# Deferring the prefix's state update of a gated-linear-attention kernel behind the next supertile's gate head

## What is computed

```python
xn = layernorm(x)
q, k, v = xn @ Wq, xn @ Wk, xn @ Wv             # 1024, 1024, 2048 wide
g = log_sigmoid(xn @ Wgk1 @ Wgk2 + bgk2) / 16   # low-rank decay gate, rank 16
# per head, in chunks: bc = cumsum(g) inside the chunk, b_last its last row
A = mask((q*exp(bc)*scale) @ (k*exp(-bc)).T)
o = A @ v + (q*exp(bc)*scale) @ S
S = S * exp(b_last) + (k*exp(b_last - bc)).T @ v
attn = (rmsnorm(o) * silu(xn @ Wg)) @ Wo
moe  = sum over the top 2 of 4 experts of  w_e * LN(relu(LN(xn @ W1_e)) @ W2_e)  + xn
out  = x + attn + moe
```

## Time and profile before

| | us |
|---|---|
| median of 2 runs | 2765.34 |
| the runs | 2757.32, 2773.36 |
| profiled execution | 2758.54 |
| its span (slowest core, core 1) | 2757.0 |
| spans of the cores | 2737.4 to 2757.0 |

### The profile page before, as it was taken

One profiled execution on the slowest core, in us unless ns is written; L12 is line 12 of the kernel. 1 busy time (PEld: TensorE's weight loads), 2 busy tenths in 40 slices (PEclk: granted clock), 3 DMA queues, 4 the chain that ended last, 5 costly groups with the idle time before them and its releaser, 6 DMA issues.

```text
span 2757.0 us, 25311 instructions; the slowest of 8 cores (2737.4 to 2757.0 us)
## 1 busy us (share of the span) xinstructions
PE 1547.7 (56%) x6272; PEld 585.3 (21%) x6272; DVE 951.4 (35%) x2139; ACT 881.1 (32%) x1617; POOL 106.9 (4%) x152
## 2 busy tenths in 40 slices
PE   1390529153788156549776662199236556966850
PEld 0140104011333012213222220044112212322310
DVE  2433343343402332333245252421233331253253
ACT  2411641063124222204453433313322212533531
POOL 1000000000000000000010000000000001000000
PEclk9595859585899588869888875599678877988975
DMA  8051226112164201027373643034310004635323
GB/s 126 0 77 31 40 39 92 31 32 31 16 92 64 44 18 21 16 37 116 55 119 65 107 63 114 23 46 67 60 27 16 16 16 69 100 66 87 57 37 122
DMA packets 258284, 155.31 MB, mean 56 GB/s; under 512 B 173016, under 2 KB 242648, under 8 KB 258144
## 3 DMA queue, kind: packets, MB, share of 16 engines
q0 software_dynamic: 84576, 94.96, 22.8%
q1 hardware_dynamic: 168960, 41.96, 8.6%
q10 hardware_dynamic: 4608, 16.78, 1.8%
HBM read 198.04 MB, written 8.39 MB: 75 GB/s over the span
## 4 chain that ended last, share of the span: by engine, by line
PE 50%; DVE 20%; DMA 11%; issue 9%; ACT 7%; DVEq 2%; SPq 1%; ACTq 0%; POOL 0%; POOLq 0%
PE pa L291 20%; PE pb L291 19%; PE pf L291 7%; DVE s_bb L546 4%; DMA s_kgT<-s_kgs 4%; DVE s_kgs L668 2%; DMA s_gx<-x_tm 2%; DMA s_ogf<-s_ogc 2%; ACT s_sg L470 2%; DVEq L64 2%; PE pd L291 1%; PE pc L291 1%; DVE s_z L926 1%; DVE s_z L932 1%; DMA s_w<-W 1%
## 5 line engine op out<-in xcount | busy, mean ns | idle before, releaser
L291 PE MATMUL pa<-s_w,s_xn 128*128 128x512 bf16 x1280 | 331.6, 406 | 391.4 <-DVE s_v L638 238.2
L291 PE MATMUL pb<-s_w,s_xn 128*128 128x512 bf16 x1280 | 313.8, 389 | 5.6 <-DMA s_w<-W 5.6
L291 PEld LDWEIGHTS pa<-s_w,s_xn 128*128 128x128 bf16 x1280 | 124.9, 102 | 562.0 <-issue 441.1
L291 PE MATMUL pf<-s_w,s_ogf 128*128 128x512 bf16 x512 | 148.5, 462 | 123.4 <-DMA s_ogf<-s_ogc 123.4
L291 PE MATMUL pa<-s_w,s_hfm 128*128 128x512 bf16 x512 | 128.2, 395 | 74.0 <-DMA s_hfm<-s_h 64.1
L765 ACT ACTIVATE s_jb<-s_ogc 128x512 bf16<-128x512 bf16 x64 | 40.3, 630 | 394.3 <-DVE s_ogc L759 392.2
L291 PEld LDWEIGHTS pb<-s_w,s_xn 128*128 128x128 bf16 x1280 | 123.2, 100 | 167.4 <-issue 39.6
L546 DVE TENSOR_TENSOR_SCAN s_bb<-c_os,s_bb 128x128 f32<-128x128 f32 x256 | 108.8, 425 | 108.7 <-ACT s_bb L539 82.8
L846 DVE TENSOR_TENSOR s_mcol<-s_scol 128x8 f32<-128x8 f32 x16 | 2.7, 167 | 405.5 <-ACT s_jb L906 404.9
L668 DVE TENSOR_SCALAR s_kgs<-s_kd,s_eb 128x128 bf16<-128x128 bf16 x256 | 65.2, 255 | 170.1 <-DMA s_kgT<-s_kgs 111.5
L291 PE MATMUL pb<-s_w,s_hfm 128*128 128x512 bf16 x512 | 122.6, 382 | 0.0
(11 more groups left out here) (176 smaller groups left out, 2264.4 us busy)
## 6 DMA issues: line engine op xcount, KB each, us to landing
s_w<-W POOLq DMA_DIRECT2D x32, 1024.0 KB, 13.8
s_w<-Wv_p POOLq DMA_DIRECT2D x8, 1024.0 KB, 20.1
s_w<-Wv POOLq DMA_DIRECT2D x8, 1024.0 KB, 16.7
s_w<-Wg POOLq DMA_DIRECT2D x8, 1024.0 KB, 13.1
s_w<-Wo POOLq DMA_DIRECT2D x8, 1024.0 KB, 12.4
s_gx<-x_tm ACTq DMA_DIRECT2D x16, 512.0 KB, 4.2
out<-s_jf ACTq DMA_DIRECT2D x16, 512.0 KB, 2.9
s_xt<-xp_tm POOLq DMA_DIRECT2D x4, 1024.0 KB, 10.7
```

Source lines behind the costliest of these rows:

```text
L291: ret = e.matmul(out=o, lhsT=l, rhs=r, start=st, stop=sp)
```

## The change

It does four things.

1. `stage_DE(True, ...)` of a prefix supertile isn't emitted at the end of its own loop round. It is held in `pend_pDE` and emitted by `emit_pend_pDE` as `mid` of the next supertile's stage B: behind the sigmoids (in m0 behind the expert gate), before Ln and the scans. In m0 it is reached through `emit_pend_G`.
2. `s_eb` gets two copies, chosen by `epar`, so that stage B of the next supertile can write its own while the old one is held.
3. `s_diag` and `s_wgk2` get places of their own (`jb_off + 4096`, `jb_off + 2048`), and the row of ones shrinks from 512 to 128 elements, of which no more were used.
4. `load_B_smalls` also waits for ScalarE, `(sc, sc.n)`; as `stage_DE` is no longer emitted ahead of it, its wait for TensorE in p1 and m0 is one for stage C.

```diff
--- before.py
+++ after.py
@@ -180,8 +180,8 @@
     s_AT = alloc("s_AT", [128, H, 128], BF16, at=jb_off + 1024)
     s_rb2 = alloc("s_rb2", [1, 1024], BF16,
                   at=big0 + attn_sz + DV * 2 + 2048)
-    s_diag = alloc("s_diag", [128, NKC, 128], BF16, at=jb_off + 2048 + 1024)
-    s_wgk2 = alloc("s_wgk2", [16, NKC, 128], BF16, at=jb_off + 2048 + 1024)
+    s_diag = alloc("s_diag", [128, NKC, 128], BF16, at=jb_off + 4096)
+    s_wgk2 = alloc("s_wgk2", [16, NKC, 128], BF16, at=jb_off + 2048)
 
     wslot = [alloc(f"s_w{i}", [128, 4096], BF16) for i in range(4)]
 
@@ -209,7 +209,7 @@
     s_cf = alloc("s_cf", [128, 1024], F32, at=si0 + 16384 + 8192)
     s_jf = alloc("s_jf", [128, 1024], F32, at=si0 + 16384 + 8192 + 4096)
 
-    s_eb = alloc("s_eb", [128, NKC, NCH], F32)
+    s_eb = alloc("s_eb", [128, 2, NKC, NCH], F32)
     s_cols = alloc("s_cols", [128, 2, 8, NTC], F32)
     s_mcol = alloc("s_mcol", [128, 2, 4, NTC], F32)
     s_gsc = alloc("s_gsc", [128, 96], F32)
@@ -225,7 +225,7 @@
     c_idb = alloc("c_idb", [128, 128], BF16)
     c_mU = alloc("c_mU", [128, 128], F32)
     c_os = alloc("c_os", [128, 128], F32)
-    c_or1 = alloc("c_or1", [1, 512], BF16)
+    c_or1 = alloc("c_or1", [1, 128], BF16)
     s_gateb = alloc("s_gateb", [1, NE], BF16)
     s_cv = alloc("s_cv", [128, 3], F32)
     assert cur[0] <= BASE + 207 * 1024, f"SBUF arena overflow: {cur[0] - BASE}"
@@ -341,7 +341,7 @@
     g_dma(c_os[:, :], onescan)
     g_dma(s_cv[:, :], cvals)
     g_dma(s_rms[:, :], rms_c)
-    g_dma(c_or1[0:1, :], onesrow)
+    g_dma(c_or1[0:1, :], onesrow[0:1, 0:128])
     g_dma(s_gateb[:, :], gatebr)
     cm = gd.n
     v_op(lambda e: e.memset(s_S[:, :, :], 0.0), wait=[(gd, cm)])
@@ -422,7 +422,7 @@
 
     def load_B_smalls(smalls, gate):
         wgk1d, wgk2d, bgk2d = smalls
-        pre = [(gd, gd.n), (te, te.n)]
+        pre = [(gd, gd.n), (te, te.n), (sc, sc.n)]
         g_dma(s_wgk1[:, :, :],
               wgk1d.rearrange("p (c n) -> p c n", n=LR), wait=pre)
         g_dma(s_wgk2[:, :, :], wgk2d.rearrange("k (c n) -> k c n", n=128))
@@ -432,7 +432,7 @@
                   gateW.rearrange("p (c n) -> p c n", n=NE))
         return gd.n
 
-    def stage_B(gw, gate, xnm, stop=None, mid=None):
+    def stage_B(gw, gate, xnm, epar=0, stop=None, mid=None):
         if stop == "Bs":
             return None, None
         if gate:
@@ -555,7 +555,7 @@
                 wait=[(ve, bbok_h)] + ([(te, te.n), (tp, tp.n)] if hf == 0 else []))
             emms.append((sc, sc.n))
             s_op(lambda e, hf=hf: e.activation(
-                out=s_eb[:, hf * 4:(hf + 1) * 4, :],
+                out=s_eb[:, epar, hf * 4:(hf + 1) * 4, :],
                 in_=s_bb[:, hf * 4:(hf + 1) * 4, 127::128],
                 func=ACT.Exp, scale=1.0 / GN))
         for hf in range(2):
@@ -649,7 +649,7 @@
                 wu_done(slot)
 
     def stage_C(prefix, eq_marks, em_marks, pre=(None, None),
-                ded=(None, None)):
+                ded=(None, None), epar=0):
         vm = (te, te.n)
         proj_tm(s_v, Wv_p if prefix else Wv, None, vm, pre_slot=pre[0],
                 ded=ded[0])
@@ -668,7 +668,8 @@
                 v_op(lambda e, kc=kc, c=c: e.tensor_scalar(
                     out=s_kgs[:, c * 128:(c + 1) * 128],
                     in0=s_kd[:, kc, c * 128:(c + 1) * 128],
-                    scalar1=s_eb[:, kc, c:c + 1], scalar2=None, op0=ALU.mult),
+                    scalar1=s_eb[:, epar, kc, c:c + 1], scalar2=None,
+                    op0=ALU.mult),
                     wait=[(ve, ve.n), (tp, prev_tp)] +
                          ([eq_marks[1], (tg[0], tg[0].n), (tg[1], tg[1].n)]
                           if (kc == 0 and c == 0) else []))
@@ -678,7 +679,7 @@
             tpms.append((tp, tp.n))
         return tpms, qbm, kbm
 
-    def stage_DE(prefix, tpms, qbm=None, kbm=None):
+    def stage_DE(prefix, tpms, qbm=None, kbm=None, epar=0):
         tp0 = tp.n
         xd0 = xd.n
         ebm = sc.n
@@ -712,7 +713,8 @@
                 if c == 0 and r == 0:
                     w0 = w0 + [(sc, ebm)]
                 v_op(lambda e, r=r, c=c: e.tensor_scalar(
-                    out=s_diag[:, r, :], in0=c_idb[:, :], scalar1=s_eb[:, r, c:c + 1],
+                    out=s_diag[:, r, :], in0=c_idb[:, :],
+                    scalar1=s_eb[:, epar, r, c:c + 1],
                     scalar2=None, op0=ALU.mult), wait=w0)
             return ve.n
 
@@ -1126,12 +1128,19 @@
         cpar_of[("m", st)] = gi % 2
         gi += 1
     xnm = stage_A(xp_tm, 0, cpar_of[("p", 0)])
+    pend_pDE = [None]
+
+    def emit_pend_pDE():
+        if pend_pDE[0] is not None:
+            stage_DE(True, pend_pDE[0][0], epar=pend_pDE[0][1])
+            pend_pDE[0] = None
     for st in range(cfg.NPST):
+        cpar = cpar_of[("p", st)]
         pv = wu_next(Wv_p[:, 0:512])
         gw_ = load_B_smalls((Wgk1_p, Wgk2_p, bgk2c_p), gate=False)
-        r_ = stage_B(gw_, gate=False, xnm=xnm)
+        r_ = stage_B(gw_, gate=False, xnm=xnm, epar=cpar, mid=emit_pend_pDE)
         eqm, emm = r_
-        tpms, qbm_, kbm_ = stage_C(True, eqm, emm, pre=(pv, None))
+        tpms, qbm_, kbm_ = stage_C(True, eqm, emm, pre=(pv, None), epar=cpar)
         sqw = [(ve, ve.n)]
         if st + 1 < cfg.NPST:
             nsrc, nt0, ncp = xp_tm, (st + 1) * ST, cpar_of[("p", st + 1)]
@@ -1140,10 +1149,11 @@
         blks = [stage_A_blk(nsrc, nt0, b, ncp, (), sq_w=sqw)
                 for b in range(NBLK)]
         xnm = stage_A_xpose(blks, (te, te.n))
-        stage_DE(True, tpms)
+        pend_pDE[0] = (tpms, cpar)
     pend_G = [None]
 
     def emit_pend_G():
+        emit_pend_pDE()
         if pend_G[0] is not None:
             stage_G(*pend_G[0])
             pend_G[0] = None
@@ -1164,15 +1174,16 @@
         r_ = stage_B(gw_, gate=True, xnm=xnm,
                      stop=stop if (stop in ("Bw1", "Bw2", "Bw3", "Bs", "B0", "B1",
                                             "B2", "B3", "B4") and st >= stop_st)
-                     else None, mid=emit_pend_G)
+                     else None, mid=emit_pend_G, epar=cpar)
         if stop in ("B", "Bw1", "Bw2", "Bw3", "Bs", "B0", "B1", "B2", "B3", "B4") \
                 and st >= stop_st:
             break
         eqm, emm = r_
-        tpms, qbm_, kbm_ = stage_C(False, eqm, emm, pre=(pv, pg2), ded=dedv)
+        tpms, qbm_, kbm_ = stage_C(False, eqm, emm, pre=(pv, pg2), ded=dedv,
+                                   epar=cpar)
         if stop == "C" and st >= stop_st:
             break
-        stage_DE(False, tpms, qbm_, kbm_)
+        stage_DE(False, tpms, qbm_, kbm_, epar=cpar)
         if stop == "D" and st >= stop_st:
             break
         side = None
```

More of the change, by code:

```diff
@@ L1232, in build @@
         pairs = [("xn", s_xn[:, :, :]), ("bb", s_bb[:, :, :]),
-                 ("eb", s_eb[:, :, :]), ("qg", s_qg[:, :, :]),
+                 ("eb", s_eb[:, 0, :, :]), ("qg", s_qg[:, :, :]),
                  ("kd", s_kd[:, :, :]), ("kgT", s_kgT[:, :, :, :]),
```

## The result

| | before | after |
|---|---|---|
| median, us | 2765.71 (10 runs) | 2796.33 (11 runs) |
| ratio, 95% interval | | 1.0131, 1.0112 to 1.015 |
| profiled execution, us | 2758.54 | 2796.95 |
| its span, us | 2757.0 (core 1) | 2795.3 (core 5) |

The changed kernel takes 1.3% longer, 31 us of median and 38 us between the profiled executions. That is less than 2%, but the interval of the ratio leaves out 1: the kernel did get slower. 2795 was forecast. The slowest core is another one in the two profiles; core 5 of the kernel before took 2756.9 us, and from here on both kernels are read on core 5, where a comparison needs the same core. Medians over few runs can hold an execution disturbed by the chip; the ratios leave these out, and where a kernel has no ratio its profiled execution is quoted.

What follows compares the result with a forecast made beforehand. TensorE's waits were read as the bound, the change touching the stretches from stage C to the next Ln. First stage A +1.5, p0/p1 +19.9, p1/m0 +14.5, m1 0: +36 on 2758.5, forecast 2795 us, range 2758 to 2812.

Steps and rivals of the forecast that it cites:

- The order: At p0/p1 and p1/m0 the update changes places with the gate head, still in series, beside no scan or V projection.
- rival 5: Update and scans overlap after all: some 40 us less at each boundary, 2680 us; chance 0.02.
- The swap: Small loads stop waiting for the update, TensorE waits for the transposes: Ln +2.9 us at p0/p1, +2.5 at p1/m0.
- The loads: Weight loads issued ahead of block 1's four transposes delay the last landing: 17 us at p0/p1, 12 at p1/m0.
- the test: The loads-plus-transposes sum tried on the old first stage A: 63.6 against 60.71 us landed, 3 us heavy.
- The sharing of the queues: DMA engines go round their queues packet by packet, so three weight loads let three transposes through; p0/p1 landing at 315.7.
- Rival 3: Level or faster: transposes come first, 2750 us, or share time evenly, 2763; chance 0.12.
- The first stage A: Small loads wait for ScalarE's Exp, weights and block 1's transposes end together: +4.3 us, corrected to +1.5.
- Rival 2: Transposes partly starved: half of 14 us won in the first stage A, boundaries lose 12 and 8; 2777 us, chance 0.18.
- m1: Small loads wait for ScalarE's end of stage F, 1633.20 for 1629.64, hidden behind the expert mix: 0 us.
- The sum: First stage A +1.5, p0/p1 +19.9, p1/m0 +14.5, m1 0: +36 us, giving 2795.
- The signs: Changed profile: wait before the head on `s_xn`, none on `s_bgk`; transposes 10 us or more; Ln near 384 and 693.

Runs made afterwards that it cites:

- overlap kernel: Changed kernel with Ln issued ahead of the update, eight scans behind each chunk's diagonal tiles, tiles and s_Em in other memory; median 2736.8 us, ratio 0.992.
- hold_all: Changed kernel with V weight loads in p0, p1 and m0 held until all eight transposes into s_xn landed; median 2752.1 us, ratio 0.9955.

## Why the prediction was right

The mechanism was the one written down, and each term came out within 2 us; the sum isn't owed to luck.

**The order.** "The update runs beside no scan and no V projection": the chain at 385 to 388 us shows it. The copies behind the scans come 45.5 us after Ln's start, as before. In the overlap kernel the order is changed, and it gains 53 us over two boundaries, where rival 5 had put some 80 on such an overlap. So rival 5 was no part of this change, and its size was too large by half, for a reason (VectorE's tiles) that the prediction didn't have.

**The swap.** 2.9 and 2.5 us were forecast from the end of one chain to the other. Between the kernel before and hold_all, 1.9 and 2.2 were measured on core 5, 2.2 and 3.4 as medians over the cores. The terms match: the gap of the small loads gone, the transposes in front. One reading was wrong: the last transpose was taken to start 1.2 us before the queue's end and to land at 297.0, but it started 2.1 us before it (292.06) and landed at 296.14, 8.2 us after the last normalisation and not 9.1. hold_all has the same 8.2.

**The loads.** 17 and 12 us were taken from a sum of 18.7 and 12.8 made lighter by what it missed on the first stage A. Changed kernel minus hold_all is 18.5 and 11.0 on core 5, and 17.5 and 11.4 over the eight cores. The correction was right in kind: from the first weight load to the last landing it was 29.5, 29.5 and 22.8 us on paper and 27.5, 27.1 and 19.9 in the trace, so the sum was 2 to 3 us heavy, as the test had said.

**The sharing of the queues.** The rule of the Trainium skill (DMA: Bandwidth & Descriptors, Queues, rings and completion order), packet for packet, fits the 2328 and 2018 packets of the contended stretch. It isn't shown by the counts that the prediction called on, since they are of stretches in which one of the two queues alone had work. Nor is the count always even: in the kernel before, core 1, it was 1731 of the weights to 907 of the transposes between 27 and 39 us, and 2391 to 3192 between 37 and 55. And whether the profile counts the packets that the page means, no run shows. Rival 3 is excluded without the rule: even shares of time would have given a landing near 301 on core 1, 13 us after the last normalisation; it came near 318 on core 5, 25.8 us after it.

**The first stage A.** +1.5 forecast, +3.3 measured: the uncorrected 4.3 was nearer. Rival 2, half of the 14 us won there, didn't happen, although block 0's transposes were free (landed by 39.3 instead of 57.5); block 1's met the loads.

**m1.** The small loads came 3.7 us later against VectorE's mark and cost nothing: the head's copy followed the expert mix at once in both kernels.

**The sum.** 1.5 + 19.9 + 14.5 = 36 against 3.3 + 20.5 + 13.1 = 36.9 on core 5, and against 3.2 + 19.7 + 14.8 = 37.7 over the eight cores, at m0's first V copy. The errors of single terms, up to 2 us, cancel in part.

**The signs.** Ln at p1 came at 387.9 and at m0 at 694.4 on core 5, forecast near 384 and 693; block 1's first three transposes took 10 to 19 us to land in p1 and m0, and the last one 8.2 and 5.4. One sign was wrong: the wait for `s_bgk` isn't gone, it is the row in front of the head (78.2 us), because the small loads land behind block 0's transposes; the wait for `s_xn` comes in the middle.

What stays open is why the stretch from m0's V to m1 scatters by 10 us between kernels. On core 5 it goes along with TensorE's busy time in it, 618 to 628 us at granted clocks of 0.83 to 0.81; on most other cores the two go together less closely.

## What to carry to other kernels

Moving a stage later in in-order queues overlaps it with nothing unless the engines' queues, and the memory that the stages share, allow it: follow the stage's last instruction on every engine and see what is queued behind. When a stage is moved, look at what its end had been holding back; here it held three weight loads (two at m0) off four transposes, and their early issue cost 29.5 us at the two boundaries while the move itself cost 2 to 6. The other 15 us that holding the loads won were lost in p0 before the change already, and 3.3 came with the added wait. Loads that are needed over 100 us later should wait for the small transfers that are needed now: on the kernel before, together with the added wait for ScalarE, this took off 0.6%.

## What the runs showed of the hardware

- Each weight load of 1 MB ahead of four DMA transposes (SBUF to SBUF) delayed the last of them by 5.6 to 6.3 us on core 5 (0, 1, 3 loads at p1: it landed 8.2, 14.1, 25.8 us after the last normalisation), also when the first load was issued only 1.4 us ahead.
- A 128x128 bf16 multiply by a column took 0.62 us on GpSimd and 0.25 us on VectorE; VectorE's scans took 0.451 us beside it and 0.425 us otherwise.
